# Starting the gathers by a count of the slots that hold rows, and moving one group's gathers out of the mixer

## Chip, cores and metric

One core of a Trainium2 chip runs the whole kernel. The metric is the device time of one execution in microseconds.

## What is computed

x is 4096 rows (2 x 2048) of 256 values. Three parts are applied in turn:

```
x = x + 0.5 * ffn(layernorm(x))
x = x + mixer(layernorm(x))
x = x + 0.5 * ffn(layernorm(x))

ffn(x):   shared = swiglu(x, shared weights)             # hidden width 512
          e      = argmax(x @ gate_w.T)                  # one of 8 experts for each row
          xs     = x * sigmoid(max(x @ gate_w.T))
          return shared + swiglu(xs, weights of e)
mixer(x): u = x @ W_in + b_in; causal conv of 4 taps over the rows, + conv_b
          h = tanh(A) h + u Bp;  y = Cp h + Dp u         # a recursion over the rows
          return silu(y) @ W_out + b_out
```

The kernel calls the two ffn parts layer one (L = 0) and layer two (L = 1).

## The kernel before

**Tiles.** The 4096 rows lie in `acc` as 32 tiles of 128 rows, in NG = 8 groups of GT = 4 tiles. Every matmul is done as three, with operands split into an upper and a lower part (`mm3`, lines 422 to 424): ScalarE makes the upper part, VectorE or GpSimd the lower.

**A layer.** TensorE does the shared expert for the first five groups of an order written out by hand, `ORDER`, (0, 7, 1, 2, 4) in layer one and (6, 7, 0, 1, 2) in layer two; then the routed experts in slots; then the shared expert for the last three, (5, 6, 3) and (3, 4, 5). For the routed part rows are sorted by expert: GpSimd scatters every row, scaled, to its place in `xs_sorted` in DRAM. Each expert gets as many slots of 128 rows as its rows need. There are NS = 39 slots (32 + 7, the most that can be needed); all 39 are always computed, those at the end that hold no row with the last expert's weights. A slot takes a load from `xs_sorted`, the expert's matmuls, a copy of y by ScalarE (line 963) into one of RING = 3 buffers, and a store to `ys_sorted` by SyncE (line 2046); buffer j counts its stores in `s_yst[j]`. Slot s uses buffer s mod 3. GpSimd loads the experts' weights (`wr_raw`, `wr_hi`, lines 1860, 1863): `wr_hi` of expert e when the last slot of expert e - 2 is finished, whose number it loads from the table `after_e` (line 1904), and then cuts `wr_lo` (line 1885). The tables are made by VectorE in `slot_tables` and `slot_experts` (lines 1291 to 1294), in the middle of the first shared group after the routing.

**The gathers.** A row's expert output comes back by an indirect DMA for each tile (line 1915), issued by GpSimd, which adds the row of `ys_sorted` to `acc`. Four of them make a group. In layer one all wait until all 39 slots are stored, `y_all_stored(0)`; in layer two the same. For the three last groups in layer two, `LATE`, the rows go to a buffer `yr` instead (line 2026), and VectorE adds them (`add_rows`, line 1438). At the very end SyncE stores each group when it is complete; group 2, gathered last, is stored last (line 2123).

**The mixer.** It runs over the groups in the order 0, 4, 1, 5, 2, 6, 3, 7; step n takes the n-th of these, and engines work two or three steps side by side. For a step: VectorE takes row statistics (`ln2_stats`, after the group's gathers), GpSimd makes the scale (`ln2_rsqrt`), ScalarE applies it (`ln2_apply`, line 996), TensorE mixes along the rows and multiplies by W_in, ScalarE and VectorE apply the conv taps (`first_tap` line 1043, `taps` line 1531) to `v`, GpSimd adds a bias (`add_bias`, line 1817), ScalarE takes silu (line 1048) and the upper part, GpSimd the lower part (`y_low`, line 1821), and TensorE multiplies by W_out. Each engine's order is written out by hand in a loop over n; instructions wait for each other by semaphores. The gathers of groups 2 and 6 come before that loop, those of group 3 at the end of GpSimd's step 0, and one tile of group 7 in each of its steps 1 to 4.

**The start of the program.** GpSimd writes zeros to all of `xs_sorted` (`zero_slots`, line 1753, five DMAs) while SyncE stores transposed x to DRAM (`xT_kept`, line 2070), for which ScalarE waits before it overwrites the source (`r1_copy`).

## Time and profile before

| | us |
|---|---|
| median of 3 runs (874.86 to 875.48) | 875.01 |
| the profiled execution | 875.05 |
| its span, first to last instruction | 873.2 |
| TensorE busy | 826.7 (95%) |
| TensorE weight loads | 722.2 (83%) |
| VectorE busy | 483.7 (55%) |
| ScalarE busy | 390.6 (45%) |
| GpSimd busy | 462.5 (53%) |

The stages by the span's clock: layer one until about 373 us (its slots from 123 to 321), the mixer until about 535, layer two's slots from about 615 to 809, its last shared groups until about 860, and the end at 873.2. Between the first and the last instruction lies the span; 1.85 us of the execution's time lie outside it. A busy share over the whole span says little here, because the stages are bound by different engines: GpSimd is idle for 40 us at a time while the slots run, and without a pause in the mixer. So what counts is read by stretches, with what each engine waited for. In the traces' rows PE is TensorE, DVE is VectorE, ACT is ScalarE, POOL is GpSimd, SP is SyncE, and a q behind the name is that engine's queue of instructions.

### The profile page before, as it was taken

The numbers are of one execution on the slowest core, as the hardware profiler recorded it, in microseconds if no ns is written. First come the engines' busy times: TensorE is split into PE (matmuls) and PEld (weight loads), VectorE is DVE, ScalarE is ACT, GpSimd is POOL, SyncE is SP. The second block draws the span as 40 slices with busy tenths as digits, with TensorE's granted clock in tenths as the row PEclk, the third lists the DMA queues.
The fourth block names the chain that finished last, engine by engine and source line by source line (L and its number), as shares of the span: only waits on it lengthen the run. The fifth ranks groups of instructions, "written<-read, shape, count | busy, mean of one in ns | idle before, by whom it ended". The sixth has DMA issues, their size and how long they took to land.

```text
span 873.2 us, 16172 instructions
## 1 busy us (share of the span) xinstructions
PE 826.7 (95%) x5302; PEld 722.2 (83%) x5303; DVE 483.7 (55%) x971; ACT 390.6 (45%) x766; POOL 462.5 (53%) x437
## 2 busy tenths in 40 slices
PE   4889999999999999999998999999999999999993
PEld 3678988888888878888887888878888888888883
DVE  7878843333333336678997886885433333333452
ACT  4643323433343434556676776233334344444330
POOL 6528860333334018889999982786331233330685
PEclk9999999999999999999999999999999999999997
DMA  7693553555554225330110015245344555521566
GB/s 266 220 329 128 169 169 121 200 184 208 177 212 155 79 87 83 43 50 12 29 40 25 25 50 194 73 141 197 121 146 180 198 196 200 185 67 37 108 152 156
DMA packets 52917, 118.15 MB, mean 135 GB/s; under 512 B 6426, under 2 KB 41380, under 8 KB 48516
## 3 DMA queue, kind: packets, MB, share of 16 engines
q0 software_dynamic: 17536, 74.33, 27.6%
q1 hardware_dynamic: 34834, 43.15, 15.0%
q8 instruction: 31, 0.51, 0.3%
q14 instruction: 18, 0.15, 0.1%
q10 hardware_dynamic: 498, 0.02, 0.0%
HBM read 83.25 MB, written 34.22 MB: 135 GB/s over the span
## 4 chain that ended last, share of the span: by engine, by line
PE 69%; POOL 13%; DVE 8%; issue 4%; DMA 3%; ACT 1%; POOLq 0%; DVEq 0%; ACTq 0%
PE bank L422 20%; PE bank L424 20%; PE bank L423 20%; POOL acc L1915 5%; PE bank L627 4%; DVE v L1531 2%; DMA wr_hi<-w_routed 2%; PE bank L596 2%; POOL v L1817 2%; POOL wr_lo L1885 2%; POOL yr L2026 1%; DVE xT_lo L1204 1%; POOL hT_lo L1821 1%; DVE hT_lo L1204 1%; PE bank L489 1%
## 5 line engine op out<-in xcount | busy, mean ns | idle before, releaser
L1885 POOL TENSOR_TENSOR wr_lo<-wr_raw,wr_hi 128x3072 fp32r<-128x3072 f32 x14 | 95.4, 6818 | 100.7 <-DMA wr_hi<-w_routed 88.9
L422 PE MATMUL bank<-wr_hi,xT_hi 128*128 x312 | 128.2, 411 | 1.5 <-POOL wr_lo L1885 1.4
L1204 DVE TENSOR_TENSOR hT_lo<-bank,hT_hi 128x512 fp32r<-128x512 f32 x78 | 54.0, 692 | 126.4 <-ACT hT_hi L879 126.4
L424 PE MATMUL bank<-wr_lo,xT_hi 128*128 x312 | 122.6, 393 | 0.0
L423 PE MATMUL bank<-wr_hi,xT_lo 128*128 x312 | 122.1, 391 | 0.0
L1489 DVE TENSOR_TENSOR hf<-sg,bank 128x512 f32<-128x512 f32 x78 | 53.7, 689 | 121.2 <-PE bank L424 121.2
L1915 POOL DMA_INDIRECT acc<-ys_sorted,pos x52 | 84.7, 1629 | 54.0 <-DMA ys_sorted<-rows 39.6
L422 PE MATMUL bank<-xT_hi,ws_hi 128*128 128x512 f32 x256 | 102.9, 402 | 3.9 <-DVE xT_lo L1204 2.6
L423 PE MATMUL bank<-xT_hi,ws_lo 128*128 128x512 f32 x256 | 100.9, 394 | 0.0
L424 PE MATMUL bank<-xT_lo,ws_hi 128*128 128x512 f32 x256 | 100.7, 393 | 0.0
L422 PE MATMUL bank<-wr_hi,hT_hi 128*128 x312 | 94.5, 303 | 3.0 <-DVE hT_lo L1204 3.0
L906 ACT ACTIVATE sg<-bank 128x512 f32<-128x512 f32 x64 | 38.2, 597 | 129.3 <-PE bank L424 117.0
L424 PE MATMUL bank<-wr_lo,hT_hi 128*128 x312 | 88.2, 283 | 0.0
L423 PE MATMUL bank<-wr_hi,hT_lo 128*128 x312 | 88.1, 282 | 0.0
L879 ACT ACTIVATE xT_hi<-bank 128x256 fp32r<-128x256 f32 (+1 forms) x102 | 43.1, 435 | 87.1 <-PE bank L596 81.0
L1300 DVE TENSOR_TENSOR hf<-sg,bank 128x512 f32<-128x512 f32 x64 | 43.6, 683 | 66.0 <-PE bank L424 51.3
L1531 DVE SCALAR_TENSOR_TENSOR v<-bank,vec,v 128x511 f32<-128x511 f32 (+2 forms) x96 | 71.0, 746 | 13.7 <-ACT v L1043 11.1
L969 ACT ACTIVATE sg<-bank 128x512 f32<-128x512 f32 x78 | 46.6, 598 | 67.9 <-PE bank L424 67.9
L422 PE MATMUL bank<-ws_hi,hT_hi 128*128 128x256 f32 x256 | 73.5, 287 | 0.2 <-DVE hT_lo L1204 0.2
L423 PE MATMUL bank<-ws_hi,hT_lo 128*128 128x256 f32 x256 | 72.4, 283 | 0.0
L424 PE MATMUL bank<-ws_lo,hT_hi 128*128 128x256 f32 x256 | 72.4, 283 | 0.0
L963 ACT ACTIVATE rows<-bank 128x256 f32<-128x256 f32 x78 | 29.9, 383 | 89.0 <-PE bank L424 89.0
(243 smaller groups left out, 2147.0 us busy)
## 6 DMA issues: line engine op xcount, KB each, us to landing
wr_raw<-w_routed POOLq DMA_DIRECT2D x16, 1536.0 KB, 7.1
wr_hi<-w_routed POOLq DMA_DIRECT2D x16, 1536.0 KB
rows<-xs_sorted SPq DMA_DIRECT2D x78, 128.0 KB, 2.6
ys_sorted<-rows SPq DMA_DIRECT2D x78, 128.0 KB, 1.7
xg<-xT_kept SPq DMA_DIRECT2D x12, 512.0 KB
xT_kept<-xTf SPq DMA_DIRECT2D x9, 512.0 KB
acc<-x SPq DMA_DIRECT2D x8, 512.0 KB, 9.8
xs_sorted<-zeros POOLq DMA_DIRECT2D x4, 1024.0 KB, 11.6
```

The costliest lines, as they stand in the source:

```text
L422: pe.matmul(o, a_hi, b_hi, start=start, stop=False, skip_group_check=True)
L423: pe.matmul(o, a_lo, b_hi, start=False, stop=False, skip_group_check=True)
L424: return pe.matmul(o, a_hi, b_lo, start=False, stop=stop, skip_group_check=True)
L879: return act.activation(o, i, ACT.Copy)
L906: act.activation(sg[:, fb % 2, :], G2[fb % 2][:, :], ACT.Silu).then_inc(s_sg, 1)
L969: act.activation(sg[:, 0, :], MG[:, :], ACT.Silu).then_inc(s_msg, 1)
L1204: return dve.tensor_tensor(o, full, f32(h), ALU.subtract)
L1300: dve.tensor_tensor(hf[:, fb % 2, :], sg[:, fb % 2, :], U2[fb % 2][:, :], ALU.mult).then_inc(s_h, 1)
L1489: dve.tensor_tensor(hf[:, 0, :], sg[:, 0, :], MU[:, :], ALU.mult).then_inc(s_mh, 1)
L1531: dve.scalar_tensor_tensor(vb_[:, d:GN], UB[cb % 2][:, 0:GN - d], vec[:, cb, k:k + 1], vb_[:, d:GN], ALU.mult, ALU.add).then_inc(s_tap if ...
L1885: pool.tensor_tensor(wr_lo[:, e % 2, :], wr_raw[:, :], f32(wr_hi[:, e % 2, :]), ALU.subtract).then_inc(s_wl, 1)
L1915: pool.indirect_dma_start(out=acc[:, tt, :], out_offset=None, in_=ys_dram, in_offset=bass.IndirectOffsetOnAxis(ap=pos[:, tt:tt + 1], axis= ...
```

## The change

- A table `y_need` of three numbers is made in `slot_experts`: 16 times the number of stores that each of the three y buffers will have seen when the last slot that holds rows is stored (a store adds 16 to its semaphore). It takes four more operations on VectorE in each layer.
- `rows_stored(L)` takes the place of `y_all_stored(L)`: GpSimd loads the three numbers one after the other and waits for each buffer's semaphore to reach it.
- In layer one the gathers of groups 0, 4 and 1 come right behind this wait; the wait for all 39 y copies and the load of `step` come behind them; then follow the gathers of groups 2 and 7, ahead of `ln2_rsqrt(0)`. Group 2's stood two groups further on, and group 7's in the mixer's steps 1 to 4.
- In the mixer only group 3 is gathered: two tiles in step 1, one in step 2, one in step 3.
- The end of `ys_sorted`, slots 32 to 38, is filled with zeros at the start, by one DMA of 896 KB from GpSimd, behind those that fill `xs_sorted`. The first `cut_part` of layer one waits for it, since `wr_lo` lies over the zeros.

```diff
             def slot_experts(src):
+                each = NS // RING
+                used = se[:, :, :].rearrange("p s e -> p (s e)")[:, 0:NS].rearrange("p (j k) -> p j k", j=RING)
+                chained(dve.tensor_tensor(used, src[0:1, E - 1:E].unsqueeze(1).to_broadcast([1, RING, each]),
+                                          sidx[:, :, :].rearrange("p (k j) a -> p j (k a)", j=RING), ALU.is_gt))
+                chained(dve.tensor_reduce(sef[:, 0:RING], used, AX.X, ALU.add))
+                chained(dve.tensor_scalar(sef[:, 0:RING], sef[:, 0:RING], 16.0, None, ALU.mult))
+                chained(dve.tensor_copy(y_need[:, :], sef[:, 0:RING]))
...
                 if i == 0:
+                    if L == 0:
+                        pool.wait_ge(s_yz, 16)
...
-            def y_all_stored(L):
+            LAST_ROWS = {1: (0, 1), 2: (2,), 3: (3,)}
+
+            def rows_stored(L):
+
+                most = 16 * (NS // RING)
                 for j in range(RING):
-                    pool.wait_ge(s_yst[j], 16 * (NS // RING) * (L + 1))
+                    need = pool.value_load(y_need[0:1, j:j + 1], min_val=16 * (NT // RING), max_val=most)
+                    wait_apart(pool, s_yst[j], need + L * most)
...
             zero_slots(ZERO_STORES - 1)
+            pool.dma_start(ys_slot[:, NT:NS, :], zeros[:, 0:NS - NT, :]).then_inc(s_yz, 16)
             pool.wait_ge(s_zero, 16 * ZERO_STORES)
...
-            y_all_stored(0)
+            rows_stored(0)
+            gather(0, s_ga[0])
+            gather(NH, s_ga[NH])
+            gather(1, s_ga[1])
             pool.wait_ge(s_ye, NS)
             pool.wait_ge(s_sst, 16)
             pool.dma_start(step[:, :, :].rearrange("p i t -> p (i t)"),
                            bass.AP(s_dram, 0, [[0, P], [1, GB * GN]])).then_inc(s_step, 16)
-            gather(0, s_ga[0])
-            gather(NH, s_ga[NH])
-            gather(1, s_ga[1])
+            gather(2, s_ga[2])
+            gather(NG - 1, s_ga[NG - 1])
             ln2_rsqrt(0)
...
             conv_bias(0)
-            gather(2, s_ga[2])
             ln2_rsqrt(2)
...
-                if 1 <= n <= GT:
-                    gather_tile(NG - 1, n - 1, s_ga[NG - 1])
+                for t in LAST_ROWS.get(n, ()):
+                    if n == 1 and t == 0:
+                        pool.wait_ge(s_add, 2 * NG)
+                    gather_tile(3, t, s_ga[3])
...
-                if n == 0:
-                    pool.wait_ge(s_add, 2 * NG)
-                    gather(3, s_ga[3])
             route_rows(1)
             experts(1)
-            y_all_stored(1)
+            rows_stored(1)
```

GpSimd, between the load of the W_in bias and the first `ln2_rsqrt`, where layer one's gathers begin; before:

```order
L1970 DMA bi_f<-b_in 1x16x32
L1974 DMA step<-step_response 128x2048 [waits m_y_copied,y_stored2,step_response_stored,y_stored1,y_stored0]
L1915 DMA acc<-ys_sorted,pos 128x256 x12
L1734 TENSOR_SCALAR ve<-mv 128x4 [waits ln2_mean_var_done]
L1737 TENSOR_TENSOR rstd<-ve,mhalf 128x4 [waits ln2_var_eps_done]
```

The same place after the change (line numbers have moved by 9 to 24):

```order
L1987 DMA bi_f<-b_in 1x16x32
L1937 TENSOR_LOAD y_need
L1937 ISA x2
L1937 TENSOR_LOAD y_need [waits y_stored0]
L1937 ISA x2
L1937 TENSOR_LOAD y_need [waits y_stored1]
L1937 ISA x2
L1926 DMA acc<-ys_sorted,pos 128x256 [waits y_stored2]
L1926 DMA acc<-ys_sorted,pos 128x256 x11
L1994 DMA step<-step_response 128x2048 [waits step_response_stored,m_y_copied]
L1926 DMA acc<-ys_sorted,pos 128x256 x8
L1743 TENSOR_SCALAR ve<-mv 128x4 [waits ln2_mean_var_done]
```

Each load of a count stands behind the wait for the buffer before it; twelve gathers are ahead of `step` and eight more ahead of `ln2_rsqrt(0)`.

GpSimd, the mixer's steps 0 and 1 (L1817 is `add_bias`, L1821 is `y_low`); before:

```order
L1817 TENSOR_TENSOR v<-v,cbs 128x512 [waits conv_bias_made,v_done] x2
L1915 DMA acc<-ys_sorted,pos 128x256 [waits shared_added]
L1915 DMA acc<-ys_sorted,pos 128x256 x3
L1821 TENSOR_TENSOR hT_lo<-v,hT_hi 128x512 [waits y_hi_done]
L1817 TENSOR_TENSOR v<-v,cbs 128x512 [waits conv_bias_made,v_done]
...
L1821 TENSOR_TENSOR hT_lo<-v,hT_hi 128x512 [waits y_hi_done]
L1817 TENSOR_TENSOR v<-v,cbs 128x512 [waits conv_bias_made,v_done]
L1915 DMA acc<-ys_sorted,pos 128x256
L1821 TENSOR_TENSOR hT_lo<-v,hT_hi 128x512 [waits y_hi_done]
```

And after:

```order
L1826 TENSOR_TENSOR v<-v,cbs 128x512 [waits conv_bias_made,v_done] x2
L1830 TENSOR_TENSOR hT_lo<-v,hT_hi 128x512 [waits y_hi_done]
L1826 TENSOR_TENSOR v<-v,cbs 128x512 [waits conv_bias_made,v_done]
...
L1830 TENSOR_TENSOR hT_lo<-v,hT_hi 128x512 [waits y_hi_done]
L1826 TENSOR_TENSOR v<-v,cbs 128x512 [waits conv_bias_made,v_done]
L1926 DMA acc<-ys_sorted,pos 128x256 [waits shared_added]
L1926 DMA acc<-ys_sorted,pos 128x256
L1830 TENSOR_TENSOR hT_lo<-v,hT_hi 128x512 [waits y_hi_done]
```

The four gathers behind step 0's two `add_bias` are gone, and step 1 has two where it had one.

VectorE, at the end of the first shared group, where the slot tables are finished; after the change (the first four rows behind `xT_lo` are new):

```order
L1206 TENSOR_TENSOR xT_lo<-xg,xT_hi 128x512 x2
L1295 TENSOR_TENSOR se<-ne,sidx 1x39
L1297 TENSOR_REDUCE sef<-se 1x3
L1298 TENSOR_SCALAR sef<-sef 1x3
L1299 CAST y_need<-sef 1x3
L1300 TENSOR_TENSOR se<-sidx,ne 1x273
L1302 TENSOR_REDUCE sef<-se 1x39
L1303 CAST slot_e<-sef 1x39
```

They stand ahead of the table of experts and of the rows that are scaled next for the scatter.

## Rows read from the trace of the kernel before

**Rows 1.** Windows of the mixer: from:to, length; busy (instructions) of each engine; clock; DMA.
```profile
383.00:470.00 87.00, 79.75 (x555) 70.44 (x553) 73.70 (x151) 61.26 (x133) 81.62 (x100) 0.98 0.12 25
...
488.00:506.00 18.00, 18.00 (x140) 16.43 (x140) 16.22 (x30) 12.34 (x24) 17.42 (x24) 1.00 0.08 30
```

**Rows 2.** Waits, 383 to 470 (total, times, longest); timeline of TensorE (start, length).
```profile
ACT v L1048 <- POOL v L1817: 18.0, 8, 5.2
...
391.71 0.80 PE L422 MATMUL bank<-xT_hi,win_hi 128*128 128x512 f32 x1 [2.17 <-DVE xT_lo L1204]
```

**Rows 3.** Timeline of GpSimd, first gather of layer one, end of `ln2_rsqrt(0)`.
```profile
324.71 1.68 POOL L1915 DMA_INDIRECT acc<-ys_sorted,pos  x1 [0.30 <-issue]
...
349.58 0.19 POOL L1763 TENSOR_SCALAR shift<-ve 128x4 f32<-128x4 f32 x1
```

**Rows 4.** Timeline of GpSimd, mixer: first and fourth gather of group 3, `add_bias(0, 2)`.
```profile
385.01 1.55 POOL L1915 DMA_INDIRECT acc<-ys_sorted,pos  x1
...
390.57 1.54 POOL L1915 DMA_INDIRECT acc<-ys_sorted,pos  x1 [0.30 <-issue]
...
392.80 1.87 POOL L1817 TENSOR_TENSOR v<-v,cbs 128x512 f32<-128x512 f32 x1
```

**Rows 5.** Timelines of ScalarE (three rows) and VectorE (one) around the mixer's start.
```profile
354.07 2.07 ACT L996 ACTIVATE xg<-acc,shift,rstd 128x256 f32<-128x256 f32 x4
...
358.81 0.60 ACT L906 ACTIVATE sg<-bank 128x512 f32<-128x512 f32 x1 [1.58 <-PE bank L424]
...
388.00 0.62 ACT L879 ACTIVATE hT_hi<-v 128x512 fp32r<-128x512 f32 x1
...
388.14 2.32 DVE L1531 SCALAR_TENSOR_TENSOR v<-bank,vec,v 128x511 f32<-128x511 f32 x3 [0.72 <-ACT v L1043]
```

**Rows 6.** Line 1863, `wr_hi` loads in each layer: min/median/max ns, first and last start.
```profile
L1863 POOL DMA_DIRECT2D wr_hi<-w_routed x6: 541/541/576, 151.6 to 265.0; - x6
...
L1863 POOL DMA_DIRECT2D wr_hi<-w_routed x6: 555/555/574, 636.5 to 758.0; - x6
```

**Rows 7.** ScalarE's y copies of slots 37 and 38, layer two; line 2046 stores there.
```profile
805.74 0.38 ACT L963 ACTIVATE rows<-bank 128x256 f32<-128x256 f32 x1 [2.20 <-PE bank L424]
...
809.37 0.38 ACT L963 ACTIVATE rows<-bank 128x256 f32<-128x256 f32 x1 [1.56 <-PE bank L424]
...
DMA to landing us min/median/max: 1.7/1.7/3.2
```

**Rows 8.** Timelines at the end: GpSimd's first and last gather, VectorE, SyncE's last store.
```profile
812.38 1.67 POOL L1915 DMA_INDIRECT acc<-ys_sorted,pos  x1 [39.59 <-DMA ys_sorted<-rows]
...
864.20 1.53 POOL L1915 DMA_INDIRECT acc<-ys_sorted,pos  x1 [0.30 <-issue]
...
861.80 1.29 DVE L1349 SCALAR_TENSOR_TENSOR acc<-bank,acc 128x512 f32<-128x512 f32 x2
...
868.24 0.37 SPq L2123 DMA_DIRECT2D out<-acc  x1
```

**Rows 9.** Line 1904, GpSimd's loads of a number from a table: min/median/max ns.
```profile
L1904 POOLq TENSOR_LOAD <-after_e x12: 284/288/516, 123.8 to 741.3; - x12
L1904 POOLq FUSED_REGOPS  x12: 147/149/191, 124.4 to 741.6; - x12
```

**Rows 10.** Timelines of VectorE (table operations) and TensorE, first shared group of layer two.
```profile
562.96 0.43 DVE L1291 TENSOR_TENSOR se<-sidx,ne 1x273 f32<-1x273 f32 x1
...
563.88 0.17 DVE L1294 CAST slot_e<-sef 1x39 int32<-1x39 f32 x1
...
571.27 0.50 PE L422 MATMUL bank<-xT_hi,ws_hi 128*128 128x512 f32 x1 [1.37 <-DVE hf L1300]
```

**Rows 11.** Line 1753, zero fills, to landing; timelines of SyncE and ScalarE beside them.
```profile
DMA to landing us min/median/max: 7.0/13.4/18.9
...
39.10 0.32 SPq L2070 DMA_DIRECT2D xT_kept<-xTf_odd  x1
...
48.08 1.08 ACT L902 ACTIVATE xTf_odd<-bank 128x512 f32<-128x512 f32 x2 [3.14 <-DMA xT_kept<-xTf_odd]
```

More of the change, by code:

```diff
@@ L122, in build @@
         slot_e = sb("slot_e", [1, NS], I32)
+        y_need = sb("y_need", [1, RING], I32)
         after_e = sb("after_e", [1, E], I32)
@@ L245, in build @@
         s_zero = sem("xs_zeroed")
+        s_yz = sem("ys_end_zeroed")
         s_st = sem("stats_done")
```

## The prediction, made before the changed kernel was run

> **What bounds the kernel now.** I read the windows first. From 383 to 470 us TensorE is busy for 79.75 of 87 us, so 7.25 us idle; from 488 on it is busy throughout [rows 1]. Then the waits of that stretch: ScalarE's silu waits eight times, 18.0 us, for `add_bias` on GpSimd; TensorE's longest stall, 2.17 us before 391.71, is another matter, since it waits for a cut of its own previous result, whatever GpSimd does [rows 2]. So up to 7.25 - 2.17 = 5.1 us of the mixer's idle TensorE hang on GpSimd, VectorE and ScalarE passing tiles around, and the gathers sit in GpSimd's queue there. Last comes the end of the program: GpSimd issues its 32 gathers of layer two without a wait from 812.38 to 865.73, the last store leaves 2.5 us later (868.24), while VectorE did its last add at 861.80 [rows 8]. The end is therefore set by GpSimd: what moves the first gather moves the end, until TensorE and VectorE come due.
>
> **How many slots hold rows.** Experts' weights are loaded when the slots of the expert two before are done: six loads of `wr_hi` in each layer, from 151.6 to 265.0 and from 636.5 to 758.0 [rows 6]. A slot takes about 4.85 us (the two last y copies aside), so these are 23 and 25 slots between the ends of expert 0 and expert 5. Routing the reference's inputs gives blocks of 4,5,4,5,4,5,5,4 = 36 in layer one and 3,6,5,4,5,5,5,5 = 38 in layer two, which agree (5+4+5+4+5 = 23, 6+5+4+5+5 = 25). Of 39 slots, three are empty in layer one and **one** in layer two.
>
> **Part 1, the tail of layer two.** The wait drops slot 38 (ring buffer 2) and keeps slot 37 (buffer 1). Their y copies on ScalarE start at 805.74 and 809.37, 3.63 us apart, and a store lands 1.7 us after its issue, 3.2 at most [rows 7]. Against that stands one new exposed step: the count of buffer 2 is loaded behind the wait for buffer 1. A load of this kind takes 0.29 us, and register work behind it 0.15 [rows 9]: 0.44. So the first gather, and with it the end, comes 3.63 - 0.44 = 3.2 us earlier. Bounds: 3.6 if the load hides, 1.7 if slot 37's store takes the longest landing (1.5 more). The first gather then starts at 809.2 and the last ends near 862.5; the last store would leave at 865.0. TensorE's side has its adds done by 863.1 and needs no gather that comes later, so it stays just inside. The Trainium skill, "DMA: Bandwidth & Descriptors", section on latency and other measured facts, puts the floor of such a load at about 600 ns, twice the row's 0.29; by it this part would be worth 2.9 and the forecast 0.3 later. The row is of this very instruction, and I keep it.
>
> **Part 2, the front of the mixer.** In layer one slots 36 to 38 drop. Two pitches of 4.85 and one of 3.63 are 13.3 us; the first gather moves from 324.71 [rows 3] to about 311, `step` no longer ahead of it. A gather costs GpSimd (390.57 - 385.01)/3 = 1.85 us [rows 4]. Twelve end near 333.5, then `step` (0.9), then eight more (14.8): GpSimd reaches `ln2_rsqrt(0)` about 349 and ends it at 351.5, where it ended at 349.77 before [rows 3]. ScalarE applies it at 354.07 and had 1.58 us of idle time before its next silu [rows 5], so 1.7 us later costs nothing. Group 5 is gathered about 1.3 us later, then group 2's four are no longer in the way, and group 6 ends near 375 instead of 381; TensorE is busy with the shared groups all this time. Cost and gain of this part: 0. The twelve gathers run beside slots 36 to 38, whose rows are already loaded; only two or three stores share the DMA engines with them, and TensorE waits for none.
>
> **Part 3, the mixer itself.** Before, four gathers of group 3 start at 385.01 behind step 0, and one of group 7 stands in each of steps 1 to 4. After: none behind step 0, two in step 1, one each in steps 2 and 3. The first four cannot be saved whole: without them GpSimd waits for y's upper half, ready at 388.62, and for VectorE's taps, ready at 390.46 [rows 5]. `add_bias(0, 2)` then ends at 390.46 + 1.28 = 391.7, before it ended at 392.80 + 1.87 = 394.67 [rows 4]: 2.9 us of lead. The second gather of step 1 takes 1.85 of it back, leaving 1.05. Steps 2 and 3 are as before. In step 4 the last gather goes, another 1.85: 1.05 + 1.85 = **2.9 us**. Since silu waits for GpSimd in every step [rows 2], the lead is passed on, and TensorE has idle time to give it back from. After 470 TensorE is the bound and keeps it. Bounds: nothing, if VectorE (73.70 of 87 us busy [rows 1]) is late in GpSimd's place; the whole 5.1 us if small stalls vanish with it.
>
> **Part 4, VectorE's four steps.** `slot_experts` gets four chained operations on one partition in each layer. The nearest rows are the table's own: 0.43 us for 273 elements and 0.17 for the last cast of 39 [rows 10], with some 0.04 of semaphore between. Three of the four have 39 elements or fewer in and out; I take 0.21 each, 0.85 together (0.8 to 1.8). In layer two they lie on the path: VectorE is behind there, and TensorE stands for 1.37 us before 571.27 until `hf` comes [rows 10]. In layer one TensorE has no such stall: 0 (up to 0.4). Cost: **0.85 us**.
>
> **Part 5, the zero fill.** 896 KB more are written behind the five fills of xs. GpSimd issues them while it waits for the fills of xs anyway. The five transfers land 7.0 to 18.9 us after issue, median 13.4 [rows 11], which is what a queue served in order gives; the sixth would then come after all of these and delay only the expert weights behind it, which are cut after the first eight scatters. The wait for it in `cut_part` is long met by then. Cost 0. The bound from above: ScalarE stood 3.14 us for the xT store issued at 39.10 and waited for until 48.08 [rows 11]; if a sixth transfer in flight took an equal share beside five, these 8.96 us would grow by a sixth, 1.5 us, straight onto TensorE. Nothing below zero is possible, as it only adds traffic.
>
> **The sum.** 875.05 (the profiled execution: 873.2 of span and 1.85 around it) - 3.2 - 2.9 + 0.85 = **869.8 us**. The median of the runs shown is 875.01, so nothing is to be shifted.
>
> **The rivals.**
> (a) *The mixer gives nothing.* VectorE's taps and cuts become what silu's chain waits for. For it: VectorE is the releaser of most small TensorE stalls and is 85% busy. Against: VectorE itself waits for ScalarE, which waits for GpSimd. 875.05 - 3.2 + 0.85 = 872.7.
> (b) *The mixer gives all.* 875.05 - 3.2 - 5.1 + 0.85 = 867.6. For it: the stalls are short and may all be echoes of one late `add_bias`; against: several are a tap finishing behind TensorE's own matmuls.
> (c) *The fill collides* with the xT store, 1.5 us on the forecast: 871.3. Against it stands the spread of the landings.
> (d) *Slower: the gathers put ahead of `ln2_rsqrt(0)` block ScalarE.* Eight gathers, 14.8 us, now stand before it. If the first gather did not start early (the count lets nothing through before slot 38, so the change does not do what it says), `ln2_rsqrt(0)` would end at 349.77 + 14.8 = 364.6. ScalarE's `ln2_apply(0)` stands in its queue ahead of the last shared group's silu; 364.6 - 354.07 - 1.58 = 8.9 us of stall for TensorE. With no gain in the tail: 875.05 + 8.9 - 2.9 + 0.85 = 881.9. It begins to cost when the first gather starts more than 4.2 us after 311 and eats all gains some 6 us later. The slot counts above speak against it.
>
> **Chances.** Forecast 0.62, (a) 0.14, (b) 0.10, (c) 0.06, (d) 0.04, and 0.04 for a mishap I don't see, half of it slower. Range: from 867.2 (case b with the load hidden) to 872.9 (case a, with a little of VectorE's steps showing in layer one too). About 0.2% of 875, 1.75 us, is what a measurement can tell from no change: faster means under 873.3. Cases (a), (b), (c) and the forecast are all faster, but (a) by only 0.6 us, and the long landing of slot 37's store would carry it over; I give half of (a) away to "same". Faster 0.87, same 0.08, slower 0.05.
>
> **What the profile of the changed kernel would show.** Part 1: the first gather of layer two about 1.4 us after slot 37's store lands, 11 slots of 4.85 us after the last `wr_hi` load as before, and the distance from first gather to end still near 61 us. If the distance from the y copy of slot 38 to the end shrinks by clearly less than 3.2, the load or the landing was mis-sized. Part 2: the first gather near 311, `ln2_rsqrt(0)` ending before 354, ScalarE's apply without a wait. Part 3: silu's waits for GpSimd well under 18.0 us, and TensorE's idle time in the 87 us near 4.5; if silu waits less and TensorE does not, (a) is it. Part 4: TensorE's stall near 571 grown by 0.85. Part 5: xT stores landing within 9 us. The prediction is wrong if GpSimd's other work does not follow its inputs as closely as I assume.

## The result: 0.28% slower, where 0.6% faster was forecast

The changed kernel took **877.73 us** in the median of 13 runs (876.42 to 880.22), the kernel before 875.48 in 13 runs beside them; the ratio is 1.0028, 95% interval 1.0020 to 1.0036, so 2.3 us slower. Forecast were 869.8 us and a range of 867.2 to 872.9. The profiled execution of the changed kernel took 879.74 us, 877.9 of it span: 2 us above its own median, and the last group of experiments says where 1.7 of them are.

ScalarE's y copies are good milestones, since there are 39 in each layer, one for each slot. The view of one line's instructions gives count, min/median/max ns, and the first and last start. The kernel before, layer one and then layer two:

```profile
L963 ACT ACTIVATE rows<-bank x39: 383/383/386, 136.2 to 321.1; 128x256 f32<-128x256 f32 x39
...
L963 ACT ACTIVATE rows<-bank x39: 383/383/386, 626.1 to 809.4; 128x256 f32<-128x256 f32 x39
```

And the changed kernel:

```profile
L965 ACT ACTIVATE rows<-bank x39: 383/383/385, 141.7 to 326.9; 128x256 f32<-128x256 f32 x39
...
L965 ACT ACTIVATE rows<-bank x39: 383/385/386, 630.7 to 814.6; 128x256 f32<-128x256 f32 x39
```

| stretch | before | changed | difference |
|---|---|---|---|
| start to layer one's first y copy | 136.2 | 141.7 | **+5.5** |
| its 39 slots | 184.9 | 185.2 | +0.3 |
| mixer, and shared groups of layer two | 305.0 | 303.8 | -1.2 |
| layer two's 39 slots | 183.3 | 183.9 | +0.6 |
| last y copy to the end | 63.8 | 63.3 | -0.5 |

The loss lies where the prediction had put nothing: in layer one's first shared groups, long before any gather. Three pieces of work meet there. `scale_rows` is VectorE's scaling of a group's rows for the scatter, `cut_part` ("the cut") is GpSimd's subtraction that makes the lower part `wr_lo` of an expert's weights, and `hf` is the hidden activation that VectorE makes and TensorE waits for. Timelines of VectorE and GpSimd there in the changed kernel (start, length; the rows at 73.82 to 74.45 are new):

```profile
73.82 0.19 DVE L1295 TENSOR_TENSOR se<-ne,sidx 1x39 f32<-1x39 f32 x1
...
74.45 0.26 DVE L1299 CAST y_need<-sef 1x3 int32<-1x3 f32 x1
...
77.14 5.40 DVE L1465 TENSOR_SCALAR more_rows<-acc,mv,rscale 128x256 f32<-128x256 f32 x8
...
80.01 2.37 POOL L1888 TENSOR_TENSOR wr_lo<-wr_raw,wr_hi 128x1024 fp32r<-128x1024 f32 x1
```

The same two pieces of work in the kernel before:

```profile
74.88 2.66 DVE L1456 TENSOR_SCALAR more_rows<-acc,mv,rscale 128x256 f32<-128x256 f32 x8
...
78.70 2.38 POOL L1877 TENSOR_TENSOR wr_lo<-wr_raw,wr_hi 128x1024 fp32r<-128x1024 f32 x1
```

`scale_rows` on VectorE (eight operations) ended at 77.54 before, 1.2 us ahead of GpSimd's cut. Now the cut starts inside it and it takes 5.40 us, twice as long: seven of the eight operations take 0.40 us as ever, and the last one 3.14, from 79.40 until 82.54, where the cut ends at 82.38.

The kernel before has such collisions too, in layer two with the same eight operations, and at 90 us in layer one with four more (1.38 us where nothing is beside them):

```profile
563.97 5.45 DVE L1456 TENSOR_SCALAR more_rows<-acc,mv,rscale 128x256 f32<-128x256 f32 x8
...
566.52 2.41 POOL L1877 TENSOR_TENSOR wr_lo<-wr_raw,wr_hi 128x1024 fp32r<-128x1024 f32 x1
```

```profile
90.45 4.17 DVE L1456 TENSOR_SCALAR rows<-acc,mv,rscale 128x256 f32<-128x256 f32 x4
...
92.05 2.41 POOL L1877 TENSOR_TENSOR wr_lo<-wr_raw,wr_hi 128x1024 fp32r<-128x1024 f32 x1
```

The one at 90 us costs TensorE nothing: it has no wait from 88 to 100 us. So a collision costs only where VectorE's late result is one that TensorE needs by then. In the changed kernel that cut starts at 92.54 and meets `hT_lo` instead, the lower part of the hidden activation: 3.80 us for two operations that took 1.47 before. That is the second of TensorE's waits. Its waits from 55 to 142 us (total, times, longest), where before had none over 0.6, and the windows (busy of each engine, granted clock, DMA share, GB/s):

```profile
PE bank L424 <- DVE hf L1309: 1.6, 1, 1.6
PE bank L424 <- DVE hT_lo L1206: 1.1, 1, 1.1
```

```profile
50.00:55.00 5.00, 5.00 (x31) 5.00 (x31) 4.79 (x13) 2.83 (x4) 0.00 (x0) 0.66 1.01 330
80.00:85.00 5.00, 3.40 (x16) 1.97 (x15) 5.00 (x6) 0.66 (x2) 4.31 (x3) 0.91 0.61 179
85.00:90.00 5.00, 5.00 (x18) 4.02 (x17) 3.82 (x11) 2.13 (x6) 3.97 (x4) 0.75 0.29 105
```

All three windows have clock 1.00 in before. Between the levels 1.2 and 2.4 GHz, 0.75 over 5 us means 2.5 us at the lower one. Either way that is 3.4 us at half clock: in the first window, and in the other two together. The 0.66 in 50 to 55 us stands ahead of the four operations, so it needs a cause of its own.

The places that the prediction spoke of went nearly as it said. ScalarE's waits from 330 to 476 us, for [rows 2]:

```profile
ACT v L1050 <- POOL v L1826: 12.8, 6, 3.3
```

Timelines of the mixer: GpSimd's first gather and the end of `ln2_rsqrt(0)`, for [rows 3]; ScalarE's apply, for [rows 5]; TensorE's stall, for [rows 2]:

```profile
316.80 1.69 POOL L1926 DMA_INDIRECT acc<-ys_sorted,pos  x1 [29.59 <-DMA ys_sorted<-rows]
...
357.23 0.19 POOL L1772 TENSOR_SCALAR shift<-ve 128x4 f32<-128x4 f32 x1
...
359.86 2.06 ACT L998 ACTIVATE xg<-acc,shift,rstd 128x256 f32<-128x256 f32 x4
...
397.50 0.50 PE L424 MATMUL bank<-xT_hi,win_hi 128*128 128x512 f32 x1 [2.12 <-DVE xT_lo L1206]
```

TensorE is 5.8 us late at 397.50 (before 391.71). Its last such stall starts a matmul at 470.47 before and at 473.44 now, 3.0 late: the mixer gave back 2.8. Silu waits for GpSimd 12.8 us in six times where it was 18.0 in eight from 324 to 470 us. Over the prediction's 87 us (here 389 to 476) TensorE is idle for 5.4 us instead of 7.25.

Layer two's table and TensorE's wait behind it, for [rows 10]:

```profile
565.74 0.19 DVE L1295 TENSOR_TENSOR se<-ne,sidx 1x39 f32<-1x39 f32 x1
...
566.66 0.43 DVE L1300 TENSOR_TENSOR se<-sidx,ne 1x273 f32<-1x273 f32 x1
...
575.09 0.50 PE L424 MATMUL bank<-xT_hi,ws_hi 128*128 128x512 f32 x1 [2.41 <-DVE hf L1309]
```

The end, for [rows 7] and [rows 8]: slot 38's y copy, GpSimd's first, thirtieth and last gather, VectorE's add of gathered rows, SyncE's last store:

```profile
814.60 0.38 ACT L965 ACTIVATE rows<-bank 128x256 f32<-128x256 f32 x1 [1.53 <-PE bank L426]
...
814.68 1.67 POOL L1926 DMA_INDIRECT acc<-ys_sorted,pos  x1 [36.92 <-issue]
...
863.22 2.50 POOL L1926 DMA_INDIRECT acc<-ys_sorted,pos  x1 [0.30 <-issue]
...
867.86 1.53 POOL L1926 DMA_INDIRECT acc<-ys_sorted,pos  x1 [0.30 <-issue]
...
863.06 1.23 DVE L1447 TENSOR_TENSOR acc<-acc,yr 128x1024 f32<-128x1024 f32 x1 [2.06 <-DMA yr<-ys_sorted,pos]
...
871.72 0.37 SPq L2140 DMA_DIRECT2D out<-acc  x1
```

The first gather starts 0.08 us after slot 38's copy, where it was 3.01: a gain of 2.93. But from first to last gather it is 53.18 us (51.82 before), and from last store to end 6.18 (4.96): 2.6 of it is gone again in this execution.

### The profile page after: what moved, and what is told of

It is laid out like the page before. It is cut to its first block, busy times and chain, and to the rows that moved or that the text cites. A ratio compares the mean times of both kernels' runs of the same rounds, so it can differ in the third digit from the quotient of the medians.

```text
span 877.9 us, 16205 instructions
## 1 busy us (share of the span) xinstructions
PE 831.4 (95%) x5302; PEld 722.7 (82%) x5303; DVE 482.7 (55%) x979; ACT 390.7 (45%) x766; POOL 465.9 (53%) x438
## 4 chain that ended last, share of the span: by engine, by line
PE 70%; POOL 11%; DVE 9%; issue 4%; DMA 3%; ACT 1%; POOLq 0%; DVEq 0%; ACTq 0%
PE bank L424 21%; PE bank L426 20%; PE bank L425 20%; POOL acc L1926 4%; PE bank L629 4%; DVE v L1540 3%; DMA wr_hi<-w_routed 2%; PE bank L598 2%; POOL v L1826 2%; POOL wr_lo L1896 1%; POOL yr L2043 1%; DVE more_rows L1465 1%; PE bank L491 1%; DMA xT_kept<-xTf_odd 1%; POOL hT_lo L1830 1%
## 5 line engine op out<-in xcount | busy, mean ns | idle before, releaser
L424 PE MATMUL bank<-wr_hi,xT_hi 128*128 x312 | 130.2, 417 | 1.0 <-POOL wr_lo L1896 1.0
L426 PEld LDWEIGHTS bank<-wr_lo,xT_hi 128*128 128x128 f32 x312 | 58.6, 188 | 14.6
```

What stands on the lines that cost most here:

```text
L424: pe.matmul(o, a_hi, b_hi, start=start, stop=False, skip_group_check=True)
L426: return pe.matmul(o, a_hi, b_lo, start=False, stop=stop, skip_group_check=True)
```

## Experiments

All ratios are to the kernel before on the same chip, whose medians were 875.0 to 875.8 us. A difference in us below is the ratio's distance from 1 times that median, which is not always the difference of the two medians (e12: 5.8 and 6.7). "First y copy" is layer one's, 136.2 us before.

| kernel | median us | ratio, 95% interval | first y copy |
|---|---|---|---|
| changed | 877.73 | 1.0028 (1.0020, 1.0036) | 141.7 |
| e1 operations alone, both layers | 881.70 | 1.0061 (1.0044, 1.0079) | 142.0 |
| e2 zero fill alone | 876.73 | 1.0008 (0.9996, 1.0020) | 135.9 |
| e3 changed, operations at the slots | 874.50 | 0.9992 (0.9979, 1.0006) | 136.8 |
| e4 order of gathers alone | 884.95 | 1.0098 (1.0080, 1.0116) | 136.2 |
| **e5 changed, count in registers** | **870.54** | **0.9949 (0.9932, 0.9966)** | 136.2 |
| e6 count in layer two alone | 872.39 | 0.9968 (0.9957, 0.9979) | 135.5 |
| e7 as e1, cut later in layer one | 879.35 | 1.0047 (1.0027, 1.0066) | 136.4 |
| e8 operations in layer two alone | 878.47 | 1.0035 (1.0023, 1.0047) | 136.0 |
| e9 as e5, cut later in layer two | 870.47 | 0.9942 (0.9929, 0.9956) | 135.9 |
| e10 as e1, cut later in both | 878.93 | 1.0041 (1.0027, 1.0055) | 136.9 |
| e11 changed, cut later in both | 873.86 | 0.9981 (0.9970, 0.9992) | 136.6 |
| e12 operations in layer one alone | 882.30 | 1.0066 (1.0047, 1.0084) | 140.1 |

### Which part loses: operations, fill or order

**e1**, the kernel before plus

```
+    used = ...
+    chained(dve.tensor_tensor(used, ..., ALU.is_gt))
+    chained(dve.tensor_reduce(sef[:, 0:RING], used, AX.X, ALU.add))
+    chained(dve.tensor_scalar(sef[:, 0:RING], sef[:, 0:RING], 16.0, None, ALU.mult))
+    chained(dve.tensor_copy(y_need[:, :], sef[:, 0:RING]))
```

> The kernel before with the four VectorE operations of the count added to both layers' slot table; the count is computed and nothing reads it; waits, gathers and fills are those of before. Theory 1 (the four operations push VectorE's first shared groups of layer one against GpSimd's cut_part): VectorE's eight scale_rows operations at 77 us take about 5.4 us with cut_part beside them where before takes 2.66, TensorE stands about 1.6 us at 84 and 1.1 us at 95, and the first y copy of layer one starts 3 to 4 us later than before's 136.2, at 139 to 140; the whole kernel is 4 to 5 us slower (layer two adds 1 to 2): about 879 to 880 us. Theory 2 (the zero fill of the end of ys costs the front of layer one): this kernel costs only 0.92 us in each layer, the first y copy at 137.1, the whole 876.5 to 877.3 us. The prediction had 0 for layer one and 0.85 for layer two: 875.9 us.

881.70 us: four operations of 0.92 us together cost 5.3 us (3.9 to 6.9). The profile repeats the changed kernel's front:

```profile
77.51 5.41 DVE L1464 TENSOR_SCALAR more_rows<-acc,mv,rscale 128x256 f32<-128x256 f32 x8
...
80.39 2.37 POOL L1885 TENSOR_TENSOR wr_lo<-wr_raw,wr_hi 128x1024 fp32r<-128x1024 f32 x1
```

**e2**, the kernel before plus

```
+    pool.dma_start(ys_slot[:, NT:NS, :], zeros[:, 0:NS - NT, :]).then_inc(s_yz, 16)
 ...
+        if L == 0:
+            pool.wait_ge(s_yz, 16)
```

> The kernel before with the zero fill of rows NT to NS of ys (896 KB on GpSimd's queue) and the wait for it in GpSimd's first cut_part, nothing else. Theory 1: the fill costs at most the 1.4 us by which the first hidden activation came later (58.69 for 57.32), and that may be the clock of that execution: the first y copy at 136.2 to 137.6, the whole 875.5 to 877 us. Theory 2: the fill carries the loss: the first y copy 3 to 5.5 us late, at 139 to 141.7, the whole 879 to 881 us, with VectorE's scale_rows at 2.66 us as before. The prediction had 0, at most 1.5.

0.7 us (-0.4 to 1.8), first y copy at 135.9. ScalarE waits for the xT store as long as in [rows 11]:

```profile
47.77 1.09 ACT L903 ACTIVATE xTf_odd<-bank 128x512 f32<-128x512 f32 x2 [3.09 <-DMA xT_kept<-xTf_odd]
```

Theory 2 falls: the fill has no part in the front. The median alone would still allow the 1.5 us of rival (c); what speaks against it is the wait of 3.09 us, which is where (c) had its cost, and the first y copy.

**e4**, the changed kernel without count, operations and fill; both layers wait for all 39 slots:

```
 def rows_stored(L):
     for j in range(RING):
-        need = pool.value_load(...)
-        wait_apart(pool, s_yst[j], need + L * most)
+        pool.wait_ge(s_yst[j], 16 * (NS // RING) * (L + 1))
```

> The changed kernel's order of gathers in layer one (groups 0, 4 and 1, the step, groups 2 and 7 ahead of the first ln2_rsqrt; group 3 in steps 1 to 3), with before's wait for all 39 slots in both layers, no count and no zero fill. By the prediction's rival with the slower end: the gathers begin where before's begin, at about 325 us, eight more of them (about 20.6 us with their step) stand ahead of the first ln2_rsqrt, ScalarE waits about 9 us for it, and of that some 6 us are left after the mixer's gain of 2.9: 878 to 882 us. If the front of the mixer has more slack than the prediction gave it, the kernel keeps the gain of 2.9: 872 to 873 us. The front of layer one is before's, the first y copy at 136.2.

884.95 us, 8.6 slower. Waits of TensorE and of ScalarE from 330 to 400 us:

```profile
PE bank L422 <- DVE hf L1300: 8.7, 1, 8.7
...
ACT xg L996 <- POOL shift L1763: 10.5, 1, 10.5
```

TensorE's stall is 8.7 us; the prediction's rival (d) had 8.9. But the 2.9 us that were to come off it did not: from layer one's last to layer two's first y copy it is 313.6 us for 305.0, so 8.6 more. Silu's waits got shorter, but TensorE's clock was 0.93 and 0.95 in 330 to 400 and 400 to 475 us, where before had 0.98 and 1.00. So the new order is a loss without the early start, and the early start is what pays for it.

### How 0.92 us becomes four or more

**e3** takes the operations out of the table and puts them ahead of the slots:

```
 def routed_slots(L):
+    stores_needed(L)
     with dve.Fori(0, NS // RING - 1) as i:
```

> The changed kernel with the four VectorE operations taken out of the slot table and put at the start of VectorE's routed slots, behind the shared groups, with a semaphore on which GpSimd waits before it reads the count. Theory 1: layer one's front goes back to before's, the first y copy at 136.2 to 137.6 us, scale_rows at 75 us again about 2.7 us; the gains in the mixer (2.9) and at the end (0.5 to 3) stay: 870 to 873 us, faster than before. Theory 2 (fill): the first y copy stays at 139 to 141.7 and the whole at 876 to 878 us, like the changed kernel.

874.50 us: the front is restored (136.8), but it is not clearly faster than before (0.7 us, -0.5 to 1.8). One reason is in the timelines of VectorE and GpSimd at the new place:

```profile
127.31 2.76 DVE L1297 TENSOR_TENSOR se<-ne,sidx 1x39 f32<-1x39 f32 x1
...
123.19 6.81 POOL L1902 TENSOR_TENSOR wr_lo<-wr_raw,wr_hi 128x3072 fp32r<-128x3072 f32 x1 [4.48 <-DVE hT_lo L1207]
```

The very operation that took 0.19 us in the table, 39 elements on one partition, takes 2.76 here: it starts 4.1 us into a cut on GpSimd and ends at 130.07, just after that cut does (130.00). In layer two it took 2.58 and ended at 618.87, behind a cut that ended at 618.80. TensorE waits 1.8 and 1.6 us for `hf` at these places (0.6 in before). TensorE's clock stayed at 1.00 behind both. Length does not scale with work here; VectorE stands until GpSimd's operation is over. The Trainium skill, "SBUF — State Buffer", section "SBUF: two separate sides", states this: GpSimd and VectorE share one pair of ports, held for a whole instruction, and a VectorE operation with two SBUF inputs (against a GpSimd one that reads SBUF), or one in a two-port mode, blocks fully until it is free. The rows of e3 agree. Whether the `scale_rows` operations run in a two-port mode no run here shows, and the held one starts 0.6 us ahead of the cut's recorded start (79.40 and 80.01). Recorded times of GpSimd are rough, and why that operation is the one to stand stays open; that it ends just behind the cut is measured.

**e7** is e1 with the cut one scatter later in layer one:

```
     in_=row_buffer(k)[:, t, :], in_offset=None).then_inc(s_sct[k % ROW_RING], 16)
+    if L == 0 and k == 2 and t == 0:
+        cut_part(L, 0)
-if k in (1, 3, 5):
+if k in (3, 5) or L and k == 1:
```

> The kernel with the four operations alone (first experiment, 881.7 us, first y copy at 142.0), with one more edit: in layer one GpSimd's first cut_part stands one scatter later, behind the first scatter of the third group, which waits for VectorE's more_rows. Theory 1a (VectorE is held by the cut that falls in its scale_rows): the eight scale_rows operations take 2.7 us again, TensorE's waits of 1.6 us at 84 and 1.1 us at 95 go, and the first y copy starts at 137 to 139.5; the whole 877 to 879 us. Theory 1b (the 0.92 us of operations delays VectorE itself, whatever GpSimd does): scale_rows may be short, but the first y copy stays at 141 to 142 and the whole at 881 to 882 us.

First y copy at 136.4 instead of 142.0. VectorE (six of the eight operations in this window; all eight take 2.66 us, until 77.81) is through before the cut:

```profile
75.80 2.01 DVE L1464 TENSOR_SCALAR more_rows<-acc,mv,rscale 128x256 f32<-128x256 f32 x6
...
79.32 2.38 POOL L1887 TENSOR_TENSOR wr_lo<-wr_raw,wr_hi 128x1024 fp32r<-128x1024 f32 x1
```

The four operations are still there, yet the front is 0.2 us later than before's, and 0.7 and 0.4 in e10 and e11, which have the same edit. So of the front's loss little is their own time; it is the collision, with what TensorE's waits and clock add. The second wait, 1.0 us for `hT_lo`, is still there in e7, so the 1.6 us wait and the 3.4 us at half clock behind it carry most. Theory 1a holds, 1b falls. The median improved by less, 1.2 us (1.0061 to 1.0047, intervals overlapping): e1's profile was the slowest of its runs and e7's the fastest of its own. Most of what e7 still loses lies in layer two, whose cut was left in its place: 1.7 us of its profile's 3.0 stand between layer one's last and layer two's first y copy.

**e8**, operations in layer two alone, and **e12**, in layer one alone:

> The kernel before with the four VectorE operations in layer two's slot table only. The prediction's fourth part: 0.85 us, 876.7 us for 875.8, TensorE's wait at 571 us 2.2 to 2.4 us for 1.37. Theory 1 as the first experiment's profile has it (6.7 us late at layer one's last y copy, 8.3 at layer two's first): 1.6 us, 877.4 us. The front of layer one is before's, the first y copy at 136.2, and TensorE's clock in 50 to 55 us is 1.00, where the two kernels with the operations in layer one had 0.66.

3.1 us (2.0 to 4.1) where the prediction had 0.85. TensorE's wait is 2.4 us for 1.4, as foreseen in size (0.85 more); but behind the longer wait its clock falls, which 1.4 us had not brought about (1.00 in both windows of before, with 3.73 and 5.00 us busy):

```profile
570.00:575.00 5.00, 2.72 (x8) 2.18 (x9) 4.81 (x11) 0.99 (x2) 3.78 (x5) 0.80 0.29 105
575.00:580.00 5.00, 5.00 (x23) 4.16 (x22) 1.55 (x3) 1.88 (x4) 4.06 (x5) 0.86 0.28 101
```

Together 1.6 us later at layer two's first y copy and 0.6 more over its slots. The latter stretch is 183.7 to 184.0 us in all kernels with the operations on VectorE (e12 too, whose layer two has none) and 183.0 to 183.3 in the others; why is open.

> The kernel before with the four VectorE operations in layer one's slot table only, the cut in its old place. The front's loss is 5.5 to 5.8 us in the two profiles that have the operations there and the cut in its old place, but 1.4 to 1.7 us of it arose ahead of the operations, with TensorE's clock at 0.66 in 50 to 55 us. Theory 1: the operations and the collision are worth 4 us, the dip of the clock comes and goes by execution: 879 us in the median for before's 875.5 (ratio 1.004 to 1.005), first y copy at 140.0 without the dip and 141.7 with it. Theory 3 (the dip belongs to this kernel as much as the collision does): clock 0.66 in 50 to 55 us again, the first y copy at 141.7 to 142, the whole 881 us (1.006). If the sum is right, layer one's share and the 3.1 us of layer two alone (1.0035) make the 5.3 us (1.0061) of both: then 2.3 us, 877.8 us.

The first y copy at 140.1 without the dip came as Theory 1 said; its 879 us did not, the median is 882.30, 5.8 us slower (4.1 to 7.4). One layer alone costs as much as both (e1: 5.3, 3.9 to 6.9). With e8's 3.1 the costs of the layers do not seem to add, though the ends of the intervals still allow it; a difference of 2.3 us for layer one was no measurement of it. The profiled execution, 881.0, has +3.9 at the front, +0.4 and +0.6 in the slots and +1.1 at the end (64.9 us from the last y copy; before itself had 63.8 in one profile and 64.8 in the other). What the slower of its runs had besides, no profile shows.

**e9, e10, e11** move layer two's cut too (e9 in layer two only), and take it out of its old place:

```
+    if k == 2 and t == 0:      # e9: only for L == 1
+        cut_part(L, 0)
```

> The kernel with the count in GpSimd's registers (870.5 us), and in layer two GpSimd's first cut_part one scatter later. In the kernel before and in all since, VectorE's eight scale_rows operations at 564 us take 5.45 us because the cut at 566.5 falls in them, and TensorE then waits 1.4 us at 571. If a cut beside scale_rows is what holds VectorE, they take 2.7 us here, the wait of 1.4 us goes, and the first y copy of layer two is 1 to 2 us earlier: 868.5 to 869.5 us. If VectorE's later operations meet the cut instead and are held as long (as the cast of bo_hl was in layer one, 1.09 to 1.72 us), the gain is 0 to 0.5 us.

Here before's own collision at 564 us goes (2.66 us for the eight operations instead of 5.45; seven of them in this window):

```profile
561.02 2.33 DVE L1457 TENSOR_SCALAR more_rows<-acc,mv,rscale 128x256 f32<-128x256 f32 x7
...
564.84 2.42 POOL L1882 TENSOR_TENSOR wr_lo<-wr_raw,wr_hi 128x1024 fp32r<-128x1024 f32 x1
```

TensorE's wait of 1.4 us went, and one of 1.0 us came at the third cut, where one `hT_lo` operation of VectorE took 3.1 us. Layer two's first y copy is 0.9 us earlier than in e5, and the ratios (0.9942, 0.9949) can't be told apart.

> The kernel with the four VectorE operations alone in both layers (881.7 us; 879.35 with the cut later in layer one), and the first cut_part one scatter later in both layers. Theory: the four operations cost by what they push together and by the clock that TensorE's waits over 1.5 us cost, hardly by their own 0.92 us: scale_rows 2.7 us in both layers, TensorE's wait at 571 to 575 us gone or under 1.4 us, its clock 1.00 in 570 to 580 us (0.80 to 0.86 with the operations in layer two and the cut in its old place): 875 to 876.5 us, within 0.2% of before. Rival: the 0.92 us is on TensorE's path in layer two by itself: 877 us or more.

The rival's price, but not by its mechanism: the operations put `scale_rows` so late in layer two that the later cut falls in it again, and nothing was moved apart. Nor does every wait over 1.5 us take TensorE's clock with it, as the expectation has it: e3's of 1.8 and 1.6 us did not.

```profile
566.23 5.44 DVE L1464 TENSOR_SCALAR more_rows<-acc,mv,rscale 128x256 f32<-128x256 f32 x8
...
569.11 2.40 POOL L1887 TENSOR_TENSOR wr_lo<-wr_raw,wr_hi 128x1024 fp32r<-128x1024 f32 x1
```

This leaves open what the 0.92 us would cost in layer two without the collision.

> The changed kernel whole, count on VectorE and all, with the one edit that the first cut_part of each layer stands one scatter later. If the collision carried the loss, the forecast of this change comes back without touching the count: before's median less 3 to 5 us, 870 to 873 us. If not, 876 to 878 us as the changed kernel.

873.86 us: the changed kernel, operations and all, becomes 1.7 us faster than before (0.7 to 2.6) by the place of the cuts. By the profile it is layer one's that does it: in layer two the collision stays, 5.43 us, with a wait of 2.3 us for `hf` behind it. That is 4.1 us from 1.0028, and the first y copy moves from 140.1 or 141.7 to 136.6.

### Whether the forecast gains are there

**e5** takes the count out of VectorE; the table `after_e` has held the number of slots with rows all along:

```
-    need = pool.value_load(y_need[0:1, j:j + 1], ...)
+slots = pool.value_load(after_e[0:1, E - 1:E], min_val=NT, max_val=NS)
+    need = (slots + (RING - 1 - j)) // RING * 16
```

> The changed kernel without the four VectorE operations and their tile: GpSimd reads the number of slots that hold rows from the table it already uses (after_e, last entry) and works out the three counts in its own registers; order of gathers and zero fill as in the changed kernel. Theory 1 (VectorE's four operations are the whole loss, the mechanisms forecast for the mixer and the end hold): the first y copy of layer one at 136.2 us, the last at 321.1, the first of layer two 2.8 to 2.9 earlier than before's at 626.1, 0.08 us from slot 38's copy to the first gather; at the end 0.5 (as in the two profiles with the count so far) to 3 us gained: 870 to 872.5 us against before's 875.8. Rival: a cost that is in neither the operations nor the fill (GpSimd's read, the waits against registers, the earlier transfers beside the last slots) holds the kernel at 874 to 876 us, as the kernel with late operations was.

870.54 us, **4.5 us faster than before** (3.0 to 6.0), 7 us better than the change as made. Milestones and the first gather of layer two:

```profile
L964 ACT ACTIVATE rows<-bank x39: 383/383/384, 136.2 to 320.7; 128x256 f32<-128x256 f32 x39
...
L964 ACT ACTIVATE rows<-bank x39: 383/383/384, 622.8 to 805.8; 128x256 f32<-128x256 f32 x39
```

```profile
805.36 1.67 POOL L1918 DMA_INDIRECT acc<-ys_sorted,pos  x1 [36.32 <-issue]
```

From layer one's last to layer two's first y copy it is 302.1 us for 305.0: 2.9, the prediction's number for the mixer. The first gather stands 0.43 us ahead of slot 38's copy, where the change's was 0.08 behind: without three loads one after the other the start gains 3.4 us instead of 2.9.

**e6** is the kernel before with e5's count in layer two alone.

> The kernel before with the count in GpSimd's registers in layer two only; layer one waits for all 39 slots, its order of gathers and everything else are before's. By the prediction's first part: 3.2 us faster (872.6 for 875.8). If the 32 gathers again take about 53.1 us where before's take 51.8, and the last store about 6.1 where before's takes 5.0, as in both profiles with the count, only 0.5 to 0.8 us is left: 875.0 to 875.3 us.

2.8 us faster (1.8 to 3.8); the prediction's first part had 3.2. In its profile the stretch from the last y copy to the end is 62.2 us, 1.6 and 2.6 shorter than in before's two profiles, though its gathers took 53.58 us.

### The dip at 50 us

**e13** and **e14** are the changed kernel again, **e15** the kernel before.

> The changed kernel once more, for its profile alone. Theory 1: if the dip of TensorE's clock in 50 to 55 us belongs to an execution, it may be absent, and then the first y copy is at 140.0 to 140.3 for 141.7 and the span 1.4 to 1.7 us shorter than 877.9; the scale_rows operations take 5.4 us either way. Theory 3: the dip is there again, and the first hf operation starts at 58.7.

> The changed kernel a third time, for its profile alone, with the same two readings: first y copy at 140.0 to 140.3 without the dip, at 141.7 with it.

> The kernel before once more, for its profile alone. Theory 1: its clock can dip in 50 to 55 us too, and then its first y copy is at 137.6 to 137.9 for 136.2; without a dip it is at 136.2. Theory 3: no dip in this kernel, the first y copy at 136.2 always. Its scale_rows operations take 2.7 us at 75 us either way.

Windows of e13, then of e14:

```profile
50.00:55.00 5.00, 5.00 (x40) 4.84 (x39) 4.79 (x13) 2.74 (x3) 0.00 (x0) 1.00 1.01 329
80.00:85.00 5.00, 3.40 (x13) 2.05 (x12) 4.92 (x10) 0.76 (x2) 3.91 (x5) 0.89 0.48 183
```

```profile
50.00:55.00 5.00, 5.00 (x30) 5.00 (x31) 4.79 (x13) 2.93 (x4) 0.00 (x0) 0.66 1.01 333
80.00:85.00 5.00, 3.39 (x15) 2.03 (x14) 5.00 (x6) 0.66 (x2) 4.43 (x4) 0.93 0.60 181
```

The dip in 50 to 55 us comes and goes with the execution of one and the same kernel: first y copy at 140.1 without it (span 876.0), 141.8 with it (878.2). A clock of 0.66 over 5 us is 3.4 us at half speed, so 1.7 us of work, the difference found. The dip at 80 to 90 us, behind the 1.6 us wait, is in both. Before (e15) showed its dip in 40 to 45 us, where TensorE waits for transfers anyway, and its first y copy at 136.0. Over all 17 profiles the dip falls in 50 to 55 us in three of the eight with the operations in layer one's table and in none of the nine others. Five more have a dip in 40 to 50 us (e6, e7, e8, e10, e15), with first y copies at 135.5 to 136.9. So such a dip comes with and without the operations; whether they have a part in its falling in 50 to 55 us, where it costs, is open. So of the 5.5 us in the first profile 1.7 are a dip that the changed kernel can also be without, and 3.9 are what stays without it (140.1 against 136.2). e13, the profile of the changed kernel without this dip, gives the plainest account of its span, 876.0 against 873.2 us: +3.9 at the front, +0.4 over layer one's slots, -1.5 from there to layer two's first y copy, +0.6 over its slots, -0.6 from the last y copy to the end.

## Why the prediction was wrong, step by step

- **How many slots hold rows**: right. The first gather of layer one starts at 316.80; the front's lag of 5.8 taken off, that is 311.0, and the forecast was 311.
- **Part 1, the tail, 3.2**: right in kind, and too large in the changed kernel. The first gather starts 2.93 earlier, and e6's median measured 2.8 (1.8 to 3.8). But the prediction's own sign was the stretch from slot 38's y copy to the end, and it shrank by 0.5 to 1.6 us only: 63.8 and 64.8 in before's two profiles, 63.2 to 63.3 in the changed kernel's three, 62.4 in e5. The load was not mis-sized (0.29 us again); wrong was that the end moves as far as the first gather. The gathers took 53.2 us from first to last in the changed kernel's three profiles, and before itself 51.82 and 52.78, so a part of this is the execution's. A gather of 1.53 us took 2.50 at 863.22, next to VectorE's add of 863.06 to 864.29; that this is the same block the other way round is only argued. From the last store to the end it is 6.0 to 6.3 us in all eight profiles with layer one's new order of gathers (e4, with before's late start, among them) and 4.9 to 5.3 in all nine without. So about 1 us at the end goes with that order; why is open.
- **Part 2, the front of the mixer, 0**: right. `ln2_rsqrt(0)` ends at 357.42, 351.6 without the lag (forecast 351.5), and ScalarE's apply doesn't wait.
- **Part 3, the mixer, 2.9**: right (2.8 in the changed kernel, 2.9 in e5). TensorE's idle time in the 87 us fell to 5.4 us, where about 4.5 was forecast. Rivals (a) and (b) fall.
- **Part 4, VectorE's four steps**: **this step failed.** Their own time was right, 0.92 for 0.85. Wrong was what they cost. "In layer one TensorE has no such stall: 0 (up to 0.4)": measured +3.9 us in the profile without the dip at 50 us, +5.5 in the one with it. I looked only for an existing stall of TensorE, and not at what the delay would bring VectorE next to. The trace of before had shown it: the same eight `scale_rows` operations in 2.66 us at 74.88, and in 5.45 at 563.97, with a cut beside them. What settles that it is the operations and the collision: without them e5 is 4.5 us faster than before, and with them but with the cut moved e11 is 1.7 us faster. In layer two "0.85" was 3.1 (2.0 to 4.1): the wait grew by 1.04 and took TensorE's clock with it.
- **Part 5, the fill, 0**: right within what can be measured (0.7, -0.4 to 1.8); ScalarE's wait, where (c) had its cost, did not grow.
- **Rival (d)**: didn't happen, since the first gather started early; its stall, 8.9, was measured in e4 as 8.7. The sum of (d) without part 4 is 6.0 us slower than before, and e4 was 8.6 slower (7.0 to 10.2), because the mixer's 2.9 did not offset the stall.

The sum with e5's costs would have been 875.05 - 3.2 - 2.9 = 868.95; measured 870.54; in e5's profile the mixer's 2.9 is whole, and the tail gave 1.4 of its 3.2. The range missed by 4.8 us at its upper end since no bound held a collision.

## What to carry to other kernels

Before a short operation is put on VectorE, look at what GpSimd runs when VectorE's next long operations come; a microsecond of delay can double them. It costs where the result behind them is one that TensorE waits for. Compare the lengths of one and the same group of operations through the trace: where one takes twice its usual time, there is a neighbour that must be kept away, and a small edit can move another group into it. A number that an engine needs can often be had from its own registers and a table that exists, at no other engine's cost.

## What the runs showed of the hardware

- A VectorE operation on 39 elements stood 2.6 to 2.8 us behind a 6.8 us GpSimd subtraction and ended 0.07 us after it, both times. Of eight that take 0.40 us each, one took 3.1 with a 2.4 us subtraction beside it, and the eight 5.4 instead of 2.66. So about all that is left of GpSimd's operation is lost, on one VectorE operation, and the rest keep their length.
- Most dips of TensorE's granted clock had the same size in these profiles: 0.66 over one window of 5 us, or split over two (0.80 and 0.86, 0.91 and 0.75), which is 3.4 us at 1.2 GHz or 1.7 us of work. Some were longer: 0.66 over the 10 us from 40 to 50 in e7, and 0.85 over the 35 us from 345 to 380 in e4, around its stall of 8.7 us, which is 6.8 and about 10 us at 1.2 GHz. In layer two none followed a wait of 1.4 us; one did after 2.4 us in e8 and the changed kernel. It is not the wait alone: e3 waited 1.8 and 1.6 us with the clock at 1.00, where 1.6 us at 80 us in the changed kernel was followed by a dip, and e13 waited 2.4 us in layer two with the clock at 1.00 throughout, and had a second wait of 1.1 us for VectorE, held by the next cut, in its place.
